# Lambda-layer block, one core: the third q product before its convolution, its loads on SyncE, two chunks of the next x among the output stores, and another table for the statistics

## What is computed

```python
xn = group_norm(x, 32 groups)                      # statistics over 16 channels and all pixels
h  = relu(bn1(conv1x1(xn, conv1_w)))               # 512 -> 128 channels
q  = bnq(conv1x1(h, q_w))                          # 64 = 4 heads x 16
k  = softmax(conv1x1(h, k_w), over pixels)         # 16
v  = bnv(conv1x1(h, v_w))                          # 32
pos = 15x15 convolution of each channel of v with emb (16 filters)
content = einsum('bkm,bvm->bkv', k, v)
h  = einsum('bhkn,bkv->bhvn', q, content) + einsum('bhkn,bkvn->bhvn', q, pos)
h  = bn3(conv1x1(relu(bn2(h)), conv3_w))           # 128 -> 512
out = x + relu(h + xn)
```

## Time and profile before

| | |
|---|---|
| median of 3 runs | 4807.04 (4805.04 to 4808.21) |
| the profiled execution's own time | 4802.3 |
| its span in the profile | 4800.5 |
| mean granted clock of TensorE | 0.959 of full |
| PE, DVE, ACT, POOL busy | 92%, 58%, 49%, 20% |

### The profile page before, as it was taken

How to read it: one execution, slowest core, us unless ns; L and a number is a source line. 1 busy time by engine, 2 the same in 40 slices (tenths; PEclk the granted TensorE clock), 3 DMA queues, 4 the chain that set the end, 5 groups by cost and what they waited for, 6 DMA issues and landing times.

```text
span 4800.5 us, 121009 instructions
## 1 busy us (share of the span) xinstructions
PE 4394.3 (92%) x49366; PEld 2693.8 (56%) x49366; DVE 2802.7 (58%) x4631; ACT 2335.2 (49%) x2880; POOL 966.8 (20%) x529
## 2 busy tenths in 40 slices
PE   4899999999999999999999999999999999999997
PEld 2555555655565655566555555555555555555554
DVE  3465655665655655556656556656566555566564
ACT  1454445454445554455544454544555544445444
POOL 0022202122211222112222121222112221112222
PEclk8899999999999999999999999999999999999998
DMA  2688778898878897788887788987888977889876
GB/s 94 212 283 288 245 269 276 277 306 271 261 270 269 283 307 256 257 277 284 282 297 245 265 278 274 304 270 249 280 271 283 306 255 252 271 269 304 267 246 246
DMA packets 537174, 1284.17 MB, mean 268 GB/s; under 512 B 43048, under 2 KB 225324, under 8 KB 528556
## 3 DMA queue, kind: packets, MB, share of 16 engines
q1 hardware_dynamic: 456396, 992.83, 63.8%
q10 hardware_dynamic: 80352, 284.45, 16.8%
HBM read 844.79 MB, written 432.33 MB: 266 GB/s over the span
## 4 chain that ended last, share of the span: by engine, by line
PE 59%; issue 12%; DMA 9%; DVE 6%; SPq 6%; POOL 4%; ACT 3%; ACTq 2%; POOLq 0%; DVEq 0%
PE ring L526 15%; PE ring L652 13%; PE ring L507 12%; PE ring L582 8%; DMA X<-x_dram 4%; DMA q_parts<-region 3%; DVE st L892 3%; PE ring L606 2%; POOL region L1191 2%; PE ring L533 2%; PE ring L616 2%; ACTq L813 2%; PE ring L538 2%; POOL X L1198 1%; SPq L402 1%
## 5 line engine op out<-in xcount | busy, mean ns | idle before, releaser
L701 ACT COPY region<-ring 126x1024 f32<-126x1024 f32 x1120 | 1103.2, 1015 | 971.7 <-PE ring L507 958.1
L582 PE MATMUL ring<-h,w3T 128*128 128x512 f32 x2048 | 991.5, 624 | 22.9 <-ACT h L720 13.2
L526 PE MATMUL ring<-X,w1e 128*128 128x512 f32 x2048 | 909.0, 597 | 3.2 <-DVE w1e L918 3.2
L652 PE MATMUL ring<-region,V 126*32 126x128 f32 x24576 | 874.9, 286 | 34.3 <-issue 34.2
L507 PE MATMUL ring<-Qt,Ep 96*126 96x256 bf16 x5120 | 759.4, 288 | 47.7 <-ACT region L701 30.8
L652 PEld LDWEIGHTS ring<-region,V 126*32 126x32 f32 x24576 | 686.1, 115 | 196.8 <-issue 191.1
L701 DVE COPY region<-ring 126x1024 f32<-126x1024 f32 x416 | 507.0, 1219 | 439.9 <-PE ring L507 416.6
L892 DVE BATCH_NORM_STATS2 st<-X 128x6 f32<-128x512 f32 x1024 | 624.7, 678 | 196.4 <-DMA X<-x_dram 196.3
L507 PEld LDWEIGHTS ring<-Qt,Ep 96*126 96x126 bf16 x5120 | 578.5, 141 | 252.9 <-issue 160.2
L526 PEld LDWEIGHTS ring<-X,w1e 128*128 128x128 f32 x2048 | 385.0, 191 | 469.6 <-issue 466.3
L582 PEld LDWEIGHTS ring<-h,w3T 128*128 128x128 f32 x2048 | 380.0, 198 | 406.1 <-issue 374.1
(11 more groups left out here) (130 smaller groups left out, 3263.4 us busy)
## 6 DMA issues: line engine op xcount, KB each, us to landing
X<-x_dram SPq DMA_DIRECT2D x132, 2048.0 KB, 20.0
out_dram<-X SPq DMA_DIRECT2D x512, 512.0 KB, 7.9
X<-x_dram ACTq DMA_DIRECT2D x124, 2048.0 KB, 10.2
V<-v_windows SPq DMA_DIRECT2D x96, 1024.0 KB, 10.9
Qt<-q_parts SPq DMA_DIRECT2D x582, 128.0 KB, 4.1
lambda_sums<-S SPq DMA_DIRECT2D x64, 1024.0 KB, 4.9
h<-lambda_sums SPq DMA_DIRECT2D x256, 256.0 KB, 5.0
q_parts<-region SPq DMA_DIRECT2D x128, 256.0 KB, 4.2
```

Of the source, the lines that this page charges most:

```text
L526: last = nc.tensor.matmul(dst[:, hh * HALF:(hh + 1) * HALF], w1e[:, c, :], X[:, j, c, hh * HALF:(hh + 1) * HALF], start=(c == 0), stop=(c ...
L582: last = nc.tensor.matmul(dst[:, yb * HALF:(yb + 1) * HALF], w3T[:, t, :], src, start=True, stop=True)
L652: last = nc.tensor.matmul(bank_of(i)[c * DV:(c + 1) * DV, (g % 4) * P:(g % 4 + 1) * P], V[0:TROWS, VSLOT[t], xb, yb * DV:(yb + 1) * DV], W ...
L701: return engine_copy(dst, src)
```

## The change

Four edits. In the mixed part q2 and k2 stand before c3, and tile o1.0 between c3 and q3. In the tail of that part the lead weights move: w0.0 and w0.1 stand behind o3.0 instead of around o2.3, and the rest follows so that the last two stand where they did. The six loads of q chunk 2 go from ACT to SP, which issues them between the stores of q chunks 2 and 3. Of the statistics, 8, 6 and 18 pieces stand in units 1, 2 and 3 (before: 8, 10, 14). And SP loads chunk 0 of the image after the next behind the loads of V, and chunk 1 behind output store 11, each once the four stores of its chunk are done; the position part loads only chunks 2 and 3.

```diff
-STATS_AT = {1: (0, 0, 0, 0, 2, 2, 2, 2), 2: (1, 1, 1, 1, 0, 2, 2, 2), 3: (2, 2, 2, 2, 2, 2, 2, 0)}
+STATS_AT = {1: (0, 0, 0, 0, 2, 2, 2, 2), 2: (1, 1, 1, 1, 0, 2, 0, 0), 3: (3, 3, 2, 2, 2, 2, 2, 2)}
...
-    order = ["c0", "nb", "c1", "q0", "k0", "o0.0", "o0.1", "c2", "q1", "k1", "o0.2", "o0.3", "c3", "q2", "k2", "q3", "k3",
-             "o1.0", "o1.1", "o1.2", "o1.3", "cl", "o2.0", "cp", "o2.1", "o2.2", "w0.0", "o2.3", "w0.1"]
-    lead = lead_names()[2:]
-    for t in range(4):
-        order += [f"o3.{t}", lead[2 * t], lead[2 * t + 1]]
-    return order
+    order = ["c0", "nb", "c1", "q0", "k0", "o0.0", "o0.1", "c2", "q1", "k1", "o0.2", "o0.3", "q2", "k2", "c3", "o1.0",
+             "q3", "k3", "o1.1", "o1.2", "o1.3", "cl", "o2.0", "cp", "o2.1", "o2.2", "o2.3", "o3.0"]
+    lead = lead_names()
+    return order + lead[0:2] + ["o3.1"] + lead[2:5] + ["o3.2"] + lead[5:8] + ["o3.3"] + lead[8:]
...
-                    for j in range(NCH):
+                    for j in range(2, NCH):
                         sp.wait_ge(out_done[j], b * (16 * CT) + HEAD)
                         load_x(b + 1, j)
...
+            def load_ahead(b, j):
+                sp.wait_ge(out_done[j], b * (16 * CT) + 16 * CT + HEAD)
+                load_x(b + 2, j)
...
                 store_out(b, 2)
+                store_out(b, 3)
                 store_q(b + 1, 2)
-                store_out(b, 3)
+                load_q(b + 1, 2)
                 store_q(b + 1, 3)
                 load_q(b + 1, 3)
                 store_v(b + 1)
                 for n in range(4, 7):
                     store_out(b, n)
                 load_v(b + 1)
-                for n in range(7, 16):
+                if ahead:
+                    load_ahead(b, 0)
+                for n in range(7, 12):
                     store_out(b, n)
+                if ahead:
+                    load_ahead(b, 1)
+                for n in range(12, 16):
+                    store_out(b, n)
...
-                    if name == "k3":
-                        load_q(b + 1, 2)
```

More of the change, by code:

```diff
@@ L450, in lam, with image @@
                 shuffle(b, 1)
-            with nc.Fori(0, B - 1, engines=OrderedEngineSet([sp.engine]), hint_back_edge=True,
-                         head_slot={sp.engine: 0}) as b:
+            def load_ahead(b, j):
+                sp.wait_ge(out_done[j], b * (16 * CT) + 16 * CT + HEAD)
+                load_x(b + 2, j)
+            def image(b, ahead):
                 lam(b, False)
@@ L469, in _ @@
                 load_v(b + 1)
-                for n in range(7, 16):
+                if ahead:
+                    load_ahead(b, 0)
+                for n in range(7, 12):
                     store_out(b, n)
+                if ahead:
+                    load_ahead(b, 1)
+                for n in range(12, 16):
+                    store_out(b, n)
+            sp.wait_ge(c_full, NCH)
+            for j in range(2):
+                load_x(1, j)
+            with nc.Fori(0, B - 2, engines=OrderedEngineSet([sp.engine]), hint_back_edge=True,
+                         head_slot={sp.engine: 0}) as b:
+                image(b, True)
+            image(B - 2, False)
             e = B - 1
@@ L807, in lead @@
                     slot(at[name], im, 0, int(name[3:]))
[L809 to L814, removed]
             def keys_out(at, im):
```

## The result

The changed kernel takes 5021.66 (median of 4 runs, 4986.36 to 5040.63) against 4807.62 of before on the same chip (4 runs, 4805.04 to 4821.63): the ratio is 1.0436 (95% interval 1.0397 to 1.0475). It is 4.4% slower. 4830 was forecast, with 4880 as the upper end.

A forecast was written before the change was run, and what follows sets the result against it. PE, busy 92%, was taken as the bound. Minus 2.54 at cp, plus 2.45 in the tail, zero for statistics and x, plus 0.85 clock: plus 0.75 a turn, 23 over 31 turns on 4807.0, so 4830; range 4765 to 4880.

The forecast's parts named there:

- The wait at cp: Mixed part: with the q loads on SP, PE no longer waits at cp for ACT's key-sum copy; minus 2.54 a turn.
- The tail: Tail of the mixed part: waits at o2.3, r0 and w0.5 go from 1.25 to 3.7, plus 2.45 a turn.
- So I cost it at nothing: Mixed part: last q loads land at 2474.1, PE reaches w0.0 at 2474.4; fits with 0.3 to spare, cost zero.
- Rival D: Mixed part: q becomes the bound and w0.0 waits; each microsecond late is 31, 4855 at 0.8; chance 0.08 inside A's.
- A: Whole kernel: waits change places and the clock falls once more often; 4830, own range 4817 to 4880; chance 0.50.
- The bytes are the same, so chunk 3 still lands when it did: x loads: DMA engines full, bytes unchanged, so chunk 3 is no later; zero, either way at most 0.2.
- nothing waits for those but loads of x: x loads: output stores finish later, but only loads of x wait for them; part of the zero, at most 0.2.
- DVE's waits for x go: x loads: DVE's waits for x vanish, but they lay in its idle time; zero, either way at most 0.2.
- The statistics: Content matmuls: the sums' wait goes, minus 1.88; a wait of 1.9 comes at w5.3 in unit 4; zero net.
- The clock: Behind the new waits at o2.3, w0.5 and w5.3: low clock follows once more often, at half price, plus 0.85 a turn.
- The order: Mixed part: q2 and k2 ahead of c3 move the same matmuls; nothing, its use being to store q2 sooner.

The follow-up runs named there:

- x_half: The changed kernel with its position-part loads of x chunks 2 and 3 moving half the bytes (output not valid): 4900.83, ratio 1.0200 to the kernel before.
- order_back: The changed kernel with only the mixed part's order put back as before, the other three edits kept: 5033.1, ratio 1.0449 to the kernel before.
- sp_q2_alone: The kernel before with only the q2 loads moved to SP and output store 3 ahead of q2's store: 4980.99, ratio 1.0348.

## Why the prediction was wrong

**The wait at cp** (minus 2.54 a turn): right. The sum of PE's idle time up to cp fell from 2.6 to 0.2, and the segment by 2.4.

**The tail** (plus 2.45): right in each place, and 0.4 short in the sum. o2.3 waits 1.65 in each turn (1.7 forecast), r0 0.64 (0.6), the weight tile behind r1 1.6 (1.4). The waits of before were taken from one image, 1.25; on the mean they were 1.0 (0.3 at o2.3), so the tail rose by 2.9.

**"So I cost it at nothing"** (q): this step failed, and it is where most of the loss began. The prediction moved six loads onto SP's queue and counted their issue time and POOL's 2.36, but not the wait that stands ahead of them: the loads wait for q2's store to land, and a wait on SP holds all that is behind it. q3's loads went out at 59.5 after nb, not at 55.3. The instruction had been read from the trace (ACT "waits there for q chunk 2 to be stored"), and the 2.9 that ACT stood was in the earlier trace rows, but it was not carried along to the engine that got the loads. Rival D had the mechanism at w0.0 with up to 1.5 a turn, and it was 1.3 in the changed kernel; it was put at a chance of 0.08 of A's. What it lacked is the rest of the queue: V, the output stores and x, all 6 to 7 later. Alone this edit costs 163, and 75 of the changed kernel's loss go if q3's store is issued ahead of the wait.

**"The bytes are the same, so chunk 3 still lands when it did"** (the x loads): failed as well. It lands at 125.3 after nb, 8.1 later than before, and the last statistics end at 130.2 instead of 125.1. The step was costed at nothing without following "nothing waits for those but loads of x" to its end: chunk 0 goes ahead of output stores, and the loads of chunks 1 to 3 wait for those. Undone this gives 50 back, made alone it costs 65, and one place later it costs nothing. But most of chunk 3's lateness is not its doing. With the x loads put back the last statistics still end at 130.9, with the q2 loads on SP as the only edit at 130.3, and with the x loads moved as the only edit at 125.6. Each as the only edit, the q2 loads on SP make chunk 3 land 6.2 later, the new order 2.5 and the moved x loads 1.6. "DVE's waits for x go" was right in part: they fell from 196.3 to 119.4 where these loads were moved alone. In the changed kernel they are 295.5:

```profile
DVE st L900 <- DMA X<-x_dram: 295.5, 90, 8.4
```

Before, nearly all of them were for chunk 0, at the start; here 203 are for chunk 1 and 90 for chunks 2 and 3, which had none.

**The statistics** (zero): the place of the new wait was right, its size was not, in both directions. With x in time it is 1.2 a turn and the edit gains 42. With x late it is 3.1 a turn (98.6 over 32), and the clock is below 0.8 behind 35 of the 59 such waits over 0.3: the low clock costs 4.6 a turn in the last part, before 1.4. That the late x is the cause, x_half shows.

**The clock** (plus 0.85): mis-placed. Behind o2.3, taken as the heir of `cp`'s low stretch, it stayed at 1.00 in every turn; behind the weight tile behind r1 it fell in 11 of 31. The stretch from cp to the content matmuls loses 0.9 to a low clock, less than the 1.4 of before. In the last part of the turn, where it was to change places only, it loses 3.2 more. In all that is 2.6 a turn.

**The order** has no cost of its own in the prediction beyond the tail. Alone it costs 58, that is 1.9 a turn. The segment behind cp grew by 2.5, about as the prediction's tail; the gain at cp was 1.0 there, since ACT still loaded q2 and the product's earlier place hardly brought its landing forward.

What stays open: the single edits sum to 30 more than the whole. That w0.0's later place hides part of q's lateness (order_back shows 6.7 against 1.3) is of the right sign and would explain more than that; how the rest divides was not measured. Nor was a kernel run in which x and q are both repaired, or one with output store 3 alone moved.

## What to carry to other kernels

A DMA that is moved to another queue takes its wait along. Write down, for each queue, when the thing waited for is done, and who is behind it; the issue time is the small part (six loads, 3.8, against 6.6 to 9.1 of standing). Move such a load behind the last instruction that need not wait for it: the same six loads cost 75 less one place later.

Full DMA engines do not make the order on them free. If loads wait for stores of their own buffer, anything put ahead of those stores delays the loads, and a landing that had 2 to spare becomes the bound of the next part.

## What the runs showed of the hardware

A store of q is two DMAs, of 256 and 128 KB. That of q0, issued at 15.9 after nb, landed at 18.2 and 19.5. That of q2 in the changed kernel, issued at 41.3 and 42.1, landed at 50.6 and 52.0, beside the 2 MB reload from ACT's queue (issued at 40.2, landed at 51.9) and output stores, at a DMA share of 0.88. Before the change, issued at 44.2 and 44.7, it landed at 48.9 and 50.6, beside the same reload from 36.4 to 48.0. The Trainium skill, "DMA: Bandwidth & Descriptors", section "Issuing engines are not separate DMA queues", says that all issuing engines' DMAs end on the same 16 DMA engines and interleave, and that issuing on several saves only the sequencer's time, usually small beside the DMA. The first half agrees with the above. The second holds here for the issue time but not for the sequencer's waiting: with ACT's queue as the one that stood for q2, the kernel took 4818, with SP's (and output store 3 ahead of q2's) 4981.

TensorE's granted clock in the stretches of 3.4 behind a wait (the length of those in the earlier trace rows), counted over all turns: 1.00 each time behind 31 waits of 1.6 to 1.7 between output tiles (512 columns); below 0.8 behind 11 of 31 waits of 1.6 between weight tiles; below 0.8 behind 21 of 31 waits at the sums (1.88 on the mean) and behind 24 of 32 at `cp` (2.54); 0.50 to 0.57 behind every one of sp_q2_alone's 32 waits for q (7.0 on the mean). Waits of equal length at two places of the same turn thus had different ends, and what makes the difference is not shown.
